# The causal mask of the transposed scores: a second TensorE product in place of GpSimd's selection

## What is computed

```python
mask = jnp.triu(jnp.full((T, T), -jnp.inf, dtype=x.dtype), k=1)[None, None]
s1 = jnp.einsum('bhtd,bhsd->bhts', q1, k1) * scale + mask
s2 = jnp.einsum('bhtd,bhsd->bhts', q2, k2) * scale + mask
a1 = jax.nn.softmax(s1, axis=-1)
a2 = jax.nn.softmax(s2, axis=-1)
```

## Time and profile before

| | us |
|---|---|
| three runs | 945.02, 946.36, 949.48 (median 946.36) |
| the profiled execution | 948.34, its span 946.6 |
| TensorE busy | 791.8 (84% of the span) |
| VectorE busy | 508.8 (54%) |
| ScalarE busy | 424.5 (45%) |
| GpSimd busy | 411.4 (43%) |
| mean granted clock of TensorE | 0.907 of 2.4 GHz |

### The profile page before, as it was taken

One profiled execution on the slowest core, in us unless ns is written; L12 is line 12 of the kernel. 1 busy time (PEld: TensorE's weight loads), 2 busy tenths in 40 slices (PEclk: granted clock), 3 DMA queues, 4 the chain that ended last, 5 costly groups with the idle time before them and its releaser, 6 DMA issues. The chain is left out here.

```text
span 946.6 us, 12914 instructions
## 1 busy us (share of the span) xinstructions
PE 791.8 (84%) x3682; PEld 386.6 (41%) x3682; DVE 508.8 (54%) x1448; ACT 424.5 (45%) x925; POOL 411.4 (43%) x753
## 2 busy tenths in 40 slices
PE   3848999889889998853695989788479999999995
PEld 2322333323323322223461223222257777777774
DVE  3748777767666765014428768672024444444445
ACT  2422555545545654511131457567314444444442
POOL 0831676425333242212221222342337677777774
PEclk9965999999999999955986799899779999999998
DMA  5485331100110110120076462232100000000001
GB/s 167 150 267 117 80 85 29 44 19 14 42 35 13 42 30 18 28 72 10 0 213 188 127 174 68 73 120 75 56 12 0 0 0 1 0 1 0 0 0 45
DMA packets 52206, 57.09 MB, mean 60 GB/s; under 512 B 13338, under 2 KB 39291, under 8 KB 52142
## 3 DMA queue, kind: packets, MB, share of 16 engines
q1 hardware_dynamic: 52148, 56.42, 21.3%
HBM read 34.70 MB, written 15.40 MB: 53 GB/s over the span
## 5 line engine op out<-in xcount | busy, mean ns | idle before, releaser
L660 ACT ACTIVATE top<-ps 128x512 f32<-128x512 f32 (+3 forms) x384 | 161.3, 497 | 156.5 <-PE ps L608 152.5
L591 PE MATMUL ps<-mid 96*128 96x512 bf16 (+3 forms) x576 | 192.3, 362 | 27.0 <-PEq L230 11.5
L608 PE MATMUL ps<-mid 99*128 99x512 bf16 (+3 forms) x576 | 182.4, 340 | 28.1 <-DMA mid<-top 9.5
L694 DVE CUSTOM_DVE_ANT_0 ps<-ps,keep 128x512 f32<-128x512 f32 (+3 forms) x384 | 183.9, 503 | 28.6 <-PE ps L591 27.4
L1374 PE MATMUL ps<-xp,wp 128*128 128x512 f32 (+1 forms) x600 | 146.9, 394 | 8.3 <-POOL wp L1467 8.3
L628 PE MATMUL ps<-top,mid 128*33 128x512 f32 (+3 forms) x768 | 150.5, 515 | 0.4 <-ACT top L660 0.4
L1374 PEld LDWEIGHTS ps<-xp,wp 128*128 128x128 f32 (+1 forms) x600 | 113.4, 189 | 34.1 <-issue 9.2
L777 POOL TENSOR_SCALAR_AFFINE_SELECT top<-top 128x128 f32<-128x128 f32 x256 | 72.4, 302 | 115.5 <-ACT top L660 110.7
L608 PEld LDWEIGHTS ps<-mid 99*128 99x128 bf16 x576 | 56.0, 100 | 152.6 <-issue 59.5
L698 DVE TENSOR_REDUCE top<-ps 128x1 f32<-128x512 f32 x128 | 88.0, 688 | 49.6 <-PE ps L591 49.6
L660 ACT ACTIVATE mid<-ps 128x512 f32<-128x512 f32 (+1 forms) x192 | 81.5, 493 | 62.2 <-PE ps L608 60.0
(11 more groups left out here) (201 smaller groups left out, 835.2 us busy)
## 6 DMA issues: line engine op xcount, KB each, us to landing
mid<-part_scratch SPq DMA_DIRECT2D x9, 1152.0 KB, 8.9
part_scratch<-top SPq DMA_DIRECT2D x18, 384.0 KB, 5.0
top<-in_w SPq DMA_DIRECT2D x16, 396.0 KB, 4.0
part_scratch<-top SPq DMA_DIRECT2D x18, 256.0 KB, 5.0
top<-inverse_scratch SPq DMA_DIRECT2D x16, 256.0 KB
mid<-part_scratch SPq DMA_DIRECT2D x9, 384.0 KB, 3.9
top<-in_w SPq DMA_DIRECT2D x8, 384.0 KB, 5.5
part_scratch<-top SPq DMA_DIRECT2D x18, 128.0 KB, 5.9
```

What stands on the lines that cost most here:

```text
L591: nc.tensor.matmul(ps[:, s_bank(turn), 0:w], queries(pair, m)[0:PARTS, i * P:(i + 1) * P], keys(pair, m)[0:PARTS, c * 512:c * 512 + w], st ...
L608: nc.tensor.matmul(ps[:, ST_BANK + n % AHEAD, 0:w], keys(pair, m)[0:STACK, j * P:(j + 1) * P], queries(pair, m)[0:STACK, q0:q0 + w], start ...
L660: nc.scalar.activation(pr[:, n % RING, 0:w], ps[:, ST_BANK + n % AHEAD, 0:w], ACT.Exp, scale=0.25).then_inc(p_ready, 1)
L694: ins = nc.vector.tensor_tensor_reduce(bank, bank, msk[:, 512 - w:512], -1.0 if low else 1.0, 3e38 if low else -3e38, ALU.add, ALU.min if ...
```

## The change

`score_step` adds the mask while the scores are still in PSUM. On a diagonal block the first product leaves the accumulation open, and a second one, with `msk[:, 384:512]` as the stationary operand and the identity `idb` as the moving one, adds the transposed triangle of -1e30 to the first 128 columns. The semaphore `st_ready` is then raised by the second product. The exponential makes 0 of these elements. GpSimd's `mask` and the semaphore `masked` go, and with them the wait in `value_step`. Later lines move by three to six numbers.

```diff
-                            nc.tensor.matmul(ps[:, ST_BANK + n % AHEAD, 0:w],
-                                             keys(pair, m)[0:STACK, j * P:(j + 1) * P],
-                                             queries(pair, m)[0:STACK, q0:q0 + w],
-                                             start=True, stop=True).then_inc(st_ready, 1)
+                            late_keys = on_diagonal(n)
+                            last = nc.tensor.matmul(ps[:, ST_BANK + n % AHEAD, 0:w],
+                                                    keys(pair, m)[0:STACK, j * P:(j + 1) * P],
+                                                    queries(pair, m)[0:STACK, q0:q0 + w],
+                                                    start=True, stop=not late_keys)
+                            if late_keys:
+                                last = nc.tensor.matmul(ps[:, ST_BANK + n % AHEAD, 0:P], msk[:, 384:512], idb[:, :],
+                                                        start=False, stop=True)
+                            last.then_inc(st_ready, 1)
...
-                            if on_diagonal(n):
-                                pe.wait_ge(masked, sum(map(on_diagonal, range(n + 1))))
...
-                        def mask(n):
-
-                            pool.wait_ge(p_ready, n + 1)
-                            square = pr[:, n % RING, 0:P]
-                            nc.gpsimd.affine_select(out=square, in_=square, pattern=[[1, P]], compare_op=ALU.is_ge,
-                                                    fill=0.0, base=0, channel_multiplier=-1).then_inc(masked, 1)
...
-                            if on_diagonal(n):
-                                mask(n)
```

More of the change, by code:

```diff
@@ L529, in attention @@
                 nm_ready, mt_ready, landed = s("nm_ready"), s("mt_ready"), s("landed")
-                cleared, masked, pch = s("cleared"), s("masked"), s("pch")
+                cleared, pch = s("cleared"), s("pch")
                 BLOCKS = N * PAIR
```

## The result

The changed kernel took 949.14 us, the median of 11 runs (948.58 to 951.72), beside 945.42 for the kernel before on the same chip (11 runs): a ratio of 1.0042, 95% interval 1.0026 to 1.0059. That is 3.7 us more, where the sum said 7.0; the interval, 2.5 to 5.6 us, leaves 7.0 out. Direction and range held. The size did not: by the prediction's own line of 0.5% (4.7 us) this is "within 0.5%", which had a chance of 0.26, and it stands nearer to rival 2 (949.7), in which the clock gives part of the cost back.

The account below looks back on a forecast made before the run. TensorE's instruction stream was taken to bound the attention loops. Layer 0's 4.7 us, layer 1's 2.1 and 0.2 for slow-clock stretches sum to 7.0, which on the median of 946.36 gives 953.4 us; range 947.2 to 961.

Parts of the forecast that it names:

- the sum: Both attention loops: the added products' cost left on TensorE's path, 7.0 us in all.
- the prediction's own line of 0.5%: Whole program: over 4.7 us is about what a measurement can tell from no change; within it, chance 0.26.
- rival 2: Clock behind long waits: masks shorten waits, two or three falls to 1.2 GHz may not come; 949.7 us, chance 0.2.
- The gain of the removal taken as 0: GpSimd's selections and the wait before 384 value products: the order hides them, so removing them gains 0.
- The price of 0.058: Each of 384 added 128-column products on TensorE: 0.058 us, with no extra for accumulating on a bank just written.
- The walk through the rounds: Pauses in TensorE's rounds of scores, maxima and value products absorb part; a head grows 0.40 us (layer 1: 0.35).
- rival 1: Mask products: nothing is absorbed, up to 968.7 us, or each costs 0.11 and pauses overflow, 963; chance 0.15.
- F: Round issuing score blocks 21 to 23 and 0 of the next head: four masks lengthen it by 0.06 us.
- The count of heads, 4.7 + 2.1: Full heads and heads shortened by transfer waits, counted: layer 0 grows 4.7 us, layer 1 2.1 us.
- Masks in stretches at 1.2 GHz, +0.2: Stretches of the loops at the lower clock: masks there cost twice, at most 0.3 us, taken as 0.2.
- the prediction's own signs: Profile after: wrong if a head grows over 0.6 us or not at all, or 1.2 GHz stretches change by over two.

Follow-up runs that it names:

- removal_only: Kernel before without GpSimd's selections and the wait on them, the causal mask left out: 947.93 us, ratio 1.0011.
- the pairs with the lead: Kernel before and changed kernel, both with spare products ahead of the loops: 946.26 and 949.54 us; with layer 0's long waits filled too: 940.99 and 946.23.
- layer1_only: Kernel before with masks by the product in layer 1 alone, by GpSimd in layer 0: 948.38 us, ratio 1.0022.
- absorbed_nine: Kernel before with only the nine masks per head that were predicted to fit into pauses done by the product: 950.55 us, ratio 1.0041.
- the filled kernels without the lead: Kernel before and changed kernel with spare products in six long waits of layer 0, none ahead of the loops: 945.36 and 945.14 us, both 0.9979.
- the two layers alone: Kernel before with masks by the product in layer 0 only, or in layer 1 only: 951.35 and 948.38 us, ratios 1.0057 and 1.0022.
- before_lead: Kernel before with one spare 512-column product behind each of the maxima products 12 to 37 ahead of either loop: 946.26 us, ratio 1.0006.

## Why the prediction was right or wrong

- **The gain of the removal taken as 0.** Right. `removal_only` has 18.32 us heads and no gain in its total. The order of the queue hid the masks, as the step said, and the 9.7 us charged to the weight load were never the product's.
- **The price of 0.058.** Right: 0.06 between starts at 2.4 GHz, and nothing extra for accumulating on a bank just written. The figure of some 81 ns of the Trainium skill (TensorE: Matmul & The Clock Gate, Back-to-back issue gap) does not hold for these products, which are 0.06 apart although each has its own weight load.
- **The walk through the rounds.** Right in each round to 0.01, and in both of its halves (0.06 for nine blocks, 0.35 for seven). (In rival 1, F at the price of 0.11 comes to 0.13 and the head to 0.99 instead of 0.97, which changes nothing.)
- **The count of heads, 4.7 + 2.1.** Supported for layer 0: 4.3 and 4.55 us in the two pairs whose loop starts at full clock, from one profile of each kernel. Open for layer 1: 0.0 as the mean of four profiles, 0.3 and 2.3 in the pairs with the lead, 2.3 by the median of `layer1_only`.
- **Masks in stretches at 1.2 GHz, +0.2.** This is the step that failed. It took the slow stretches as given and let the masks cost double in them; to meet the measured 3.7 the term would have to be -3.1. The runs showed that the stretches themselves depend on the added work. TensorE's time at 1.2 GHz, from a loop's first score to its last, was 26.3 us in layer 0 without the mask products and 20.2 with them, and in layer 1 22.0 and 14.5 (means of the four profiles each that the layers' lengths were taken from). In these profiles the loops grew by 3.8 us and not by 6.8. In layer 0, 0.9 is missing, and the first two heads account for it (1.0). In layer 1, 2.1 is missing; the first head accounts for some 1.3 (1.0 shorter, where 0.35 longer was forecast), and the rest lies in heads whose waits for transfers differ by up to 3 us between executions. That the clock gave back all of the 3.3 us is therefore argued and not shown. By the prediction's own signs it was wrong too: the stretches at 1.2 GHz in the two loops went from 10 to 7, by more than two.
- **Rival 2.** Its size was right, 949.7 against 949.14, and its place only in part, so that the size is in part luck. The stretches at 1.2 GHz behind the waits at the transposed maxima, from 254.5 and 336.4 in the kernel before, are gone in the changed one, as it said: the four profiles without the products in layer 0 have six such stretches, the four with them none. But the last one, behind the wait before the maxima rows, is twice as long (6.8 us from 363.1, against 3.4). And about half of the time at 1.2 GHz that went (3.6 of 6.1 us in layer 0, 3.3 of 7.5 in layer 1) lies at the starts of the two loops, which it did not mention. All eight profiles of each layer agree on that part. A product in TensorE's stream is both a cost and activity, and where the stream is thin the second can outweigh the first. The Trainium skill (TensorE: Matmul & The Clock Gate, What's actually happening) says that activity releases the throttled state. The first heads agree: 16 more products, and 1.2 us less.
- **The chances.** 0.2 for this rival was low. The kernel before had a mean clock of 0.907 and five slow stretches in layer 0 besides its start, in view. That showed how much there was to return.

**What stays open.** The three measurements of the whole change (3.7 to 3.8 us) and the two layers alone (7.5 together) differ by somewhat more than their intervals allow (some 3 us). Why `absorbed_nine` costs 3.9 us with heads that grow by 0.06 and a clock that rose, why the filled kernels without the lead were level, why the lead brought nothing by itself, and what the masks cost in layer 1, no run settles. The first two speak against the account as far as they go. Executions of one kernel differ by up to 10 us (943.4 to 953.4 in 29 runs of the kernel before), and in them a clock lower by 0.001 goes with a time longer by 0.6 to 0.85 us. That is a correlation; which of the two leads was not tested.

## What to carry to other kernels

Cost an added instruction on the bounding engine by its distance of starts, round by round, with the pauses that take it in. Here that held to 0.01 us a head. Then add a term of its own for the clock: list the stretches of the kernel before at the lower clock and ask of each whether the change makes the stream ahead of it denser or thinner. And test such a term by taking away all that the clock can return in both versions. Taking away one part of it proved nothing here: with the starts alone at full clock the masks still cost 3.3 us, and with the waits alone filled they cost nothing.

## What the runs showed of the hardware that was not expected

- More work on TensorE raised its granted clock over the whole program, from 0.9085 to 0.9175 with 384 products of 0.06 us, and products whose results are thrown away raised it to 0.933. Put ahead of both loops and into the six waits of layer 0, they made the kernel 5.2 us faster (0.9943 [0.9922, 0.9964]).
- An earlier return to 2.4 GHz need not shorten the program. `before_lead` had 0.924 instead of 0.909 and the same time; in its layer 1, ScalarE waited 4.48 us instead of 3.30 for the same transfers.
- GpSimd's 107 us of selections, which read and wrote the tiles that TensorE then used, slowed neither TensorE nor VectorE: with and without them VectorE was busy 12.91 us in a full head, and TensorE's products kept their distances.
